# Adding key tiles of an attention denominator: vector instructions of GpSimd, or accumulating DMA transfers that GpSimd issues

## The reference

```python
g = jnp.clip(_bn(conv1x1(l, w_inside)), 0.0, 6.0)
theta = l[:, :32]
f = jnp.einsum('niab,nicd->nabcd', theta, theta)          # 3136 x 3136 scores of an image
f = jax.nn.softmax(f.reshape(n, h * w, h, w), axis=1)      # over the first pixel
f = jax.nn.softmax(f.reshape(n, h * w, h * w), axis=2)     # over the second pixel
out = jnp.einsum('nabcd,nicd->niab', f, g) / h * w
out = depthwise3x3(out); out = _bn(out) + l
```

## Time and profile before

| | us |
|---|---|
| median of three runs | 5719.85 |
| profiled execution | 5723.8 |
| its span, first to last instruction | 5721.9 |
| PE / ACT / DVE / POOL busy | 5287.3 / 5129.3 / 4463.7 / 4668.5 |
| mean granted clock of TensorE | 0.957 of full speed |
| queue of SyncE's DMAs: share of 16 engines | 31.4% |

### The profile page before, as it was taken

How to read it: one execution, slowest core, us unless ns; L and a number is a source line. 1 busy time by engine, 2 the same in 40 slices (tenths; PEclk the granted TensorE clock), 3 DMA queues, 4 the chain that set the end, 5 groups by cost and what they waited for, 6 DMA issues and landing times.

```text
span 5721.9 us, 90179 instructions
## 1 busy us (share of the span) xinstructions
PE 5287.3 (92%) x32898; PEld 2681.3 (47%) x32898; DVE 4463.7 (78%) x8965; ACT 5129.3 (90%) x3029; POOL 4668.5 (82%) x1913
## 2 busy tenths in 40 slices
PE   8999969989989898989898989899898989898995
PEld 3444435445545454545454544445454545454442
DVE  7888858878878787878787878788787878787875
ACT  7888859989989898989898989899898989898984
POOL 5666635888988888888888889889888888888885
PEclk9999969999999999999999999999999999999997
DMA  7887742222222222222222222122222222222211
GB/s 149 159 164 162 150 81 53 54 48 51 42 44 58 58 58 58 58 58 58 58 58 54 60 52 51 46 49 43 51 58 58 58 58 58 58 58 58 58 35 35
DMA packets 231221, 382.47 MB, mean 67 GB/s; under 512 B 161981, under 2 KB 179582, under 8 KB 220542
## 3 DMA queue, kind: packets, MB, share of 16 engines
q1 hardware_dynamic: 230782, 376.70, 31.4%
HBM read 260.16 MB, written 103.56 MB: 64 GB/s over the span
## 4 chain that ended last, share of the span: by engine, by line
PE 40%; POOL 17%; issue 11%; SPq 7%; ACT 6%; DMA 4%; DVE 3%; POOLq 0%; DVEq 0%
PE at_AV L963 21%; PE at_S L932 12%; POOL at_OUTB L758 6%; PE at_AV L969 5%; POOL at_ZP L745 5%; POOL at_ZB L756 3%; ACT at_ring L781 3%; ACT at_ring L787 3%; SPq L653 2%; DMA zd<-at_ZACC 2%; DVE at_ring L836 2%; PE at_AV L959 1%; SPq L629 1%; DMA rzd<-at_ZC 1%; POOL at_OUTB L760 1%
## 5 line engine op out<-in xcount | busy, mean ns | idle before, releaser
L836 DVE TENSOR_SCALAR_CACHE_REDUCE at_ring<-at_S 128x1176 f32<-128x1176 f32 (+1 forms) x2352 | 2889.8, 1242 | 322.1 <-PE at_S L932 294.2
L745 POOL TENSOR_TENSOR at_ZP<-at_ZP,at_ring 128x1568 f32<-128x1568 f32 x704 | 2505.1, 3601 | 381.9 <-ACT at_ring L787 350.5
L781 ACT ACTIVATE at_ring<-at_ring,at_NM 128x3136 f32<-128x3136 f32 x784 | 2278.0, 2906 | 380.3 <-DVE at_NM L845 375.0
L963 PE MATMUL at_AV<-at_ring,at_GT 128*64 128x392 f32 x12800 | 2352.3, 508 | 46.3 <-issue 39.5
L787 ACT ACTIVATE at_ring<-at_ring,at_RZ 128x3136 f32<-128x3136 f32 x784 | 2274.1, 2901 | 0.7 <-DVE at_RZ L853 0.7
L932 PE MATMUL at_S<-at_THM,at_THS 128*128 128x392 f32 x6144 | 1492.7, 371 | 307.9 <-DVE at_ring L836 264.3
L932 PEld LDWEIGHTS at_S<-at_THM,at_THS 128*128 128x128 f32 x6144 | 1043.7, 192 | 994.9 <-DVE at_ring L836 716.4
L963 PEld LDWEIGHTS at_AV<-at_ring,at_GT 128*64 128x64 f32 x12800 | 875.2, 139 | 1180.9 <-issue 1093.3
L758 POOL TENSOR_TENSOR at_OUTB<-at_OUTB,at_ZB 128x1568 f32<-128x1568 f32 x248 | 885.7, 3572 | 16.9
L969 PE MATMUL at_AV<-at_ring,at_ones 128*32 128x392 f32 x6656 | 618.5, 498 | 0.0
L458 DVE TENSOR_TENSOR l_U<-l_TY,l_XB 128x448 f32<-128x448 f32 x896 | 497.0, 617 | 99.4 <-PE l_TY L498 99.2
(11 more groups left out here) (70 smaller groups left out, 2520.5 us busy)
## 6 DMA issues: line engine op xcount, KB each, us to landing
l_X<-in_x SPq DMA_DIRECT2D x128, 392.0 KB, 7.5
at_THM<-hld SPq DMA_DIRECT2D x128, 392.0 KB, 7.5
at_THS<-hld SPq DMA_DIRECT2D x256, 192.0 KB, 4.3
at_CIN<-att SPq DMA_DIRECT2D x64, 406.0 KB, 7.6
at_ZB<-rzd SPq DMA_DIRECT2D x64, 406.0 KB, 4.9
yd<-l_YO SPq DMA_DIRECT2D x128, 196.0 KB, 5.5
att<-at_ACC SPq DMA_DIRECT2D x256, 98.0 KB
at_OUTB<-yd SPq DMA_DIRECT2D x64, 392.0 KB, 8.9
```

The source lines that it names most:

```text
L745: e.tensor_tensor(z, z, v, ALU.add).then_inc(g_add, 1)
L781: e.activation(v, v, ACT.Exp, bias=NM[:, i:i + 1], accum_out=ZS[:, i:i + 1]).then_inc(a_p1, 1)
L836: e.tensor_scalar(ring[:, s % RING, QC * a_:QC * b].rearrange("p (b w) -> p b w", w=QC), PS[:, k % 2, 0:b - a_, 0:QC], 1.0, None, ALU.mult ...
L963: ins = e.matmul(dst[64 * j:64 * j + 64, 0:QC], GT[fl.n % 2][:, keys_of(fl.n, t), :], ring[:, slot, q:q + QC], start=(t == GROUPS[fl.i][0] ...
```

## The change

GpSimd no longer adds with vector instructions. For the first of the twelve tiles it issues a plain DMA transfer from the ring's buffer to ZP, for the other eleven a transfer that adds its source to what stands in ZP (`accum_op=ALU.add`), each over the whole tile (1.606 MB), cut into two rows of 1568 elements for each partition. Each adds 16 to `g_add` when it has landed, and each but the first of an image waits until the one before it has landed. The first waits for the second z fill of group 5 of the image before. The plan counts 1.5 us of GpSimd for an issue and 9.0 us to the landing.

```diff
-    adds = [(n, t, h) for n in range(n_img) for t in POOLED for h in range(2)]
+    adds = [(n, t) for n in range(n_img) for t in POOLED]
...
             if t == POOLED[0] and n:
-                free = summed.get((n - 1, h), inf) + LAT
+                free = summed.get((n - 1, 1), inf) + LAT
+            elif n or t != POOLED[0]:
+                free = end_add[n, POOLED[POOLED.index(t) - 1]] + LAT
...
-                tg = end_add[n, t_, h] = t + (1700 if t_ == POOLED[0] else 3600)
+                tg, end_add[n, t_] = t + 1500, t + 9000
...
-            return 2 * (len(POOLED) * n + POOLED.index(t)) + h + 1
+            return 16 * (len(POOLED) * n + POOLED.index(t) + 1)
...
-            def add(n, t, h):
+            def add(n, t):
                 s = base(n) + t
-                v = ring[:, s % RING, HW // 2 * h:HW // 2 * (h + 1)]
-                z = ZP[:, HW // 2 * h:HW // 2 * (h + 1)]
                 e.wait_ge(a_p2, s + 1)
                 if t == POOLED[0]:
                     if n:
-                        e.wait_ge(pe_f, index["z", n - 1, POOLED_IN, h] + 1)
-                    e.tensor_copy(z, v).then_inc(g_add, 1)
+                        e.wait_ge(pe_f, index["z", n - 1, POOLED_IN, 1] + 1)
+                    e.dma_start(ZP[:, :], ring[:, s % RING, :]).then_inc(g_add, 16)
                 else:
-                    e.wait_ge(g_add, added(n, t, h) - 2)
-                    e.tensor_tensor(z, z, v, ALU.add).then_inc(g_add, 1)
+                    e.wait_ge(g_add, added(n, t) - 16)
+                    e.dma_start(ZP[:, :], ring[:, s % RING, :], max_dma_last_dim=2 * HW, accum_op=ALU.add).then_inc(g_add, 16)
...
                 if t == SUM:
-                    e.wait_ge(g_add, added(fl.n, POOLED[-1], fl.j))
+                    e.wait_ge(g_add, added(fl.n, POOLED[-1]))
```

## The result

| | before | after |
|---|---|---|
| median of three runs, us | 5719.85 | 6505.36 (6492.08 to 6515.57) |
| ratio, with its 95% interval | | 1.137 (1.134 to 1.141) |
| span of the profiled execution, us | 5721.9 | 6503.5 |
| mean granted clock of TensorE | 0.957 | 0.907 |

The change makes the kernel 786 us slower. 5530 was predicted, and the range ended at 6050.

A forecast was written before the change was run, and what follows sets the result against it. GpSimd's convolution was taken to hold SyncE's queue, so sums landed late and ScalarE lost time. From 5723.8 us, minus 247 and 5, plus 62 for TensorE's wait: 5534, as median 5530; range 5450 to 6050.

The forecast's parts named there:

- What bounds the kernel: GpSimd's convolution holds SyncE's queue, which delays the sum's store and VectorE's line 890; gain 269 us gross, 252 net.
- full gain: Rival: T at or under 8.75 us, no wait at TensorE's sum over ZP, 5468 us; chance 0.13.
- W = 4T - 35: TensorE's wait per image before the sum over ZP: 3 us, less 1 for its lead, 62 us over 31 images.
- 94 us stand against 59 + 4T: Convolution start to TensorE's ZP sum, 94 us, must cover the 59 us convolution and four additions behind it.
- T: One addition by transfer, from its issue to its landing, taken as 9.5 us.
- two-pass value, 10.7: Landing time of one addition if the transfer also reads its destination, two passes at 371 GB/s: 10.7 us.
- 4T - 36: TensorE's wait per image at the ZP sum after its lead; slower from 8.0 us, at T = 11.0.
- 12T + 4: Image period in us if the chain of twelve additions sets it, should the cover beside ScalarE go.
- the queue takes over: Rival: T at 15.5 us, the additions set a period of 190 us an image, 6900 us; chance 0.11.
- The sum that comes late: Rival: TensorE's line 969 waits on ZP, 4 us an image per microsecond of T, 5730 to 6050 us; chance 0.22.
- The store that stays late: Rival: the sum's store queues behind an addition in flight, up to T more, 5640 us; chance 0.06.
- Hidden work: First tile's copy and additions 1 to 13 lie beside ScalarE; transfers fill the engines 90 us of each 146.

The follow-up runs named there:

- kernel without additions: The kernel before, with GpSimd only copying the first tile into ZP and the other eleven left out of the sum: 5451.17 us.
- middle four: The changed kernel with only tiles 8, 9, 12 and 13 added by DMA transfer and the other eight by GpSimd's vector instructions: 5452.65 us.
- store later: The kernel before, with the output's store moved in SyncE's list behind the next image's loads and the sum's store: 5450.11, then 5456.64 us (median of four).
- The copies: The changed kernel with plain copies in place of the accumulating transfers, same bytes and order, additions left out: 5736.11 us.

## Why the prediction was wrong

**What bounds the kernel: right.** The loop from the convolution through SyncE's queue to line 890 was there, and its price was 261 us of ScalarE's time by the kernel without additions, where 269 gross and 252 net stood. Three kernels (no additions, middle four, store later) lie between 5450 and 5457; the rival of full gain gave 5468.

**GpSimd's side: nearly right.** An issue takes 1.21 us (1.5 taken, 0.3 to 1.9 bounds), the convolution 59 to 63 us (59). SyncE's wait for it fell by almost half (2777.6 us in 30 images to 1489.8 in 29) but not to nothing, and the wait at line 890 by 219 us, to 64, a little over the 60 named. What was not seen is that SyncE itself gets slower: the eight issues of the sum's store, which take 2.5 us in the images of the kind of the earlier trace rows, take 6.7 to 9.2 there now, here 9.02:

```profile
2050.77 9.02 SPq L660 DMA_DIRECT2D zd<-at_ZACC  x8
```

**The step that failed: W = 4T - 35, from "94 us stand against 59 + 4T".** It gave 2 us an image; 29.9 stand there. Taking it apart at its own terms, in means of both kinds of image: from the convolution's start to the sum pass 112.9 us, 54.7 of them the last four additions, so T is 13.7 and not 9.5. Against the 92.6 before that makes 20.3. The other 9.9 us are the convolution's start, which comes that much later than before against ScalarE's tile 8; the prediction had it 3 us earlier in one kind. 20.3 + 9.9 = 30.2.

*T*: 9.5 + 1.5 + 0.5 + 2.2 = 13.7. The fixed part of 2.0 us is right, 2.0 here. The 16 packets were priced too low, at 7.5 us (9.5 - 2.0), and take 9.0. The prediction's own two-pass value, 10.7, lies near the 11.0 of an undisturbed addition; the 1.2 us that it took off, for a write beside the second read, had no row and did not show. A link has 0.6 us between a landing and the next issue, three times in four additions, 0.5 for each addition. And 2.2 us are collisions with SyncE's transfers: in the means tile 17 lands after 17.0 us, tile 16 after 13.5 and tile 19 after 11.4, in place of 11.0. The share of 0.00 in the earlier trace rows that stood for an idle queue was a stretch of one image; the loads for the next image fall on the last four additions of each.

Packets fill 9.0 us of an undisturbed addition and 5.4 of a copy, 1.7 times; the quicker packets alone take about 500 and 250 ns, twice. By the rule of the Trainium skill that the prediction quoted ("Collectives: The Full Stack", section on the bandwidth ceiling), that a second source read halves the rate, the trace agrees for the quicker packets, and over a whole transfer it shows less than that; no run shows the read itself. The estimate of 9.4 us from "DMA: Bandwidth & Descriptors" is 1.6 under the undisturbed 11.0, all of it in the bytes, since its fixed 2.0 us agree; the measurement decides.

*Only the last four were counted.* A larger T alone does not give the time: by the prediction's own 4T - 36, T = 13.7 makes 18.8 us an image and 5468 + 31 x 18.8 = 6051 us, 454 short of the measured time. The prediction held the first eight additions for hidden and had the chain of twelve as a far limit, "12T + 4". This limit is what binds. In the kernel in which the sum reads another tile the period is the twelve links alone, 12 x 13.4 = 160.5 us, over the 143.3 of an image without additions. Where the sum waits too, the 4 us behind the last landing are in truth 14.0: the next image's first tile is made only after TensorE goes on. So the rival "the queue takes over" had the right loop and put it too far away, at T = 13: already 12T + 4 reaches 143.3 at T = 11.6. The copies bear it out: 3.7 us less in each transfer gave 25 us an image, 6.7 times as much and not four times.

**The other rivals.** The sum that comes late was the mechanism on the losing side, and TensorE's row shows it as described, but its price of 4 us for each microsecond of T leaves out the loop. The store that stays late behind an addition in flight: in part, 64 us. Hidden work, forecast at nothing: the first eight additions are not hidden, and their packets fill not 12 x (T - 2) = 90 but 101 us of an image (0.499 x 6503.5 / 32).

What was not settled: how the 9.9 us of the later start divide between SyncE's slow issues, the slower loads of the convolution's input (12.4 us to landing, 7.6 before) and the chain itself; the kernel without convolution shows only that the chain is enough.

## What to carry to other kernels

Work that is moved into a chain of dependent transfers must be priced as a loop: every link from issue to next issue, collisions with other loads included, times all links of a period, plus what must happen before the first link can start again, and held against the period and not against the last wait. And before work is taken off an engine that a queue waits for, look whether the waiting instruction can stand elsewhere in its queue: here one line of SyncE's list gave 4.6%, with the engine as busy as ever.

## What the runs showed of the hardware

- A transfer of 1.6 MB within SBUF, two rows a partition and nothing beside it, lands after 11.0 us when it adds to its destination and after 7.3 when it does not. A packet of 6272 bytes takes 562 and 338 ns in the mean, quicker and slower ones by turns (about 500 and 620 ns, 250 and 420). What is not packets is 2.0 and 1.9 us, and 1.8 for an addition of half the size.
- The issue costs GpSimd 1.21 us with accumulation and 0.74 without (1.6 MB in two rows a partition; means of 352), and the instruction behind it is stretched: line 756 takes 2.04 us right behind an issue and 1.58 else.
- SyncE's issues stretch beside GpSimd's transfers: eight that follow each other took 2.5 us in every second image and take 6.7 to 9.2.
- TensorE's granted clock fell to 0.50, its lower level of 1.2 GHz, while it stood 29.5 us, and the sum's eight matmuls behind the wait took 1.53 us against 0.84; from 2211 us on it was 1.00 again. Windows of the kernel after (length, the engines PE to POOL, then clock, DMA share, GB/s):

```profile
2178.00:2204.00 26.00, 0.00 (x0) 0.00 (x0) 0.00 (x0) 2.44 (x1) 2.41 (x2) 0.55 0.89 170
2205.00:2206.60 1.60, 1.53 (x9) 0.27 (x9) 0.00 (x0) 0.00 (x0) 0.00 (x0) 0.50 0.00 0
...
2211.00:2216.00 5.00, 5.00 (x29) 2.38 (x30) 4.46 (x10) 5.00 (x3) 0.00 (x0) 1.00 0.06 14
```
